# Delta-rule layers: v copied to SBUF by ScalarE, k and q projected to exchanged PSUM banks

## The reference, cut to what matters

```python
def delta_rule(q, k, v, beta):
    def step(W, inp):
        qt, kt, vt, bt = inp
        wk = einsum('bhde,bhe->bhd', W, kt)
        v_new = bt * (vt - wk)
        W = W + einsum('bhd,bhe->bhde', v_new, kt)
        return W, einsum('bhde,bhe->bhd', W, qt)

def fast_ff(x, ln_g, ln_b, slow_w, out_w):
    h = layer_norm(x, ln_g, ln_b)
    q, k, v, beta = split(h @ slow_w.T)          # 8 heads of 64, beta one per head
    q, k, beta = softmax(q), softmax(k), sigmoid(beta)
    return x + delta_rule(q, k, v, beta) @ out_w.T
```

## Time and profile before

| | us |
|---|---|
| median of 3 runs (lowest to highest) | 3078.03 (3076.59 to 3078.49) |
| the profiled execution | 3075.59 |
| its span, first to last instruction | 3073.70 |
| VectorE busy in the span | 2118.2 (69%) |
| TensorE busy in the span | 2422.8 (79%) |
| ScalarE busy in the span | 1209.8 (39%) |
| GpSimd busy in the span | 654.5 (21%) |

### The profile page before, as it was taken

One profiled execution on the slowest core, in us unless ns is written; L12 is line 12 of the kernel. 1 busy time (PEld: TensorE's weight loads), 2 busy tenths in 40 slices (PEclk: granted clock), 3 DMA queues, 4 the chain that ended last, 5 costly groups with the idle time before them and its releaser, 6 DMA issues. The chain is left out here.

```text
span 3073.7 us, 43978 instructions
## 1 busy us (share of the span) xinstructions
PE 2422.8 (79%) x16426; PEld 1407.0 (46%) x16426; DVE 2118.2 (69%) x4507; ACT 1209.8 (39%) x1941; POOL 654.5 (21%) x632
## 2 busy tenths in 40 slices
PE   6757777777659999977888888777688888876598
PEld 2232222222234444335666666543466666665343
DVE  2347888888946777748888888612788888883332
ACT  4555444545423222243444444234343443441332
POOL 0004555555500000022222222101322222220000
PEclk9878888888879999988888988778798989986699
DMA  1000000000010000002222222210122222220000
GB/s 34 1 9 1 0 0 0 1 0 1 0 42 0 0 1 0 26 11 42 42 39 40 36 39 42 39 25 1 32 42 43 43 42 43 43 41 12 16 1 27
DMA packets 280817, 65.88 MB, mean 21 GB/s; under 512 B 272968, under 2 KB 274464, under 8 KB 280224
## 3 DMA queue, kind: packets, MB, share of 16 engines
q1 hardware_dynamic: 280608, 63.09, 11.0%
HBM read 44.20 MB, written 18.86 MB: 21 GB/s over the span
## 5 line engine op out<-in xcount | busy, mean ns | idle before, releaser
L907 POOL TENSOR_TENSOR ma_hc<-ma_state,ma_c 128x508 f32<-128x508 f32 x256 | 302.1, 1183 | 370.9 <-DVE ma_state L994 186.2
L2079 DVE TENSOR_TENSOR fw_lane_x<-fw_lane_x,fw_lane_p 128x126 f32<-128x126 f32 (+22 forms) x992 | 330.6, 333 | 34.0
L994 DVE TENSOR_TENSOR_SCAN ma_state<-ma_da,ma_ps_dbx 128x510 f32<-128x510 f32 x256 | 311.5, 1217 | 32.6 <-issue 24.1
L2075 DVE TENSOR_TENSOR fw_lane_p<-fw_lane_a,fw_lane_x 128x126 f32<-128x126 f32 (+22 forms) x992 | 273.5, 276 | 29.6
L1658 PE MATMUL fw_p<-fw_w,fw_xs 128*127 128x512 f32 (+1 forms) x512 | 238.2, 600 | 54.0 <-DVE fw_qk L2059 26.3
L809 PE MATMUL ma_ps_y<-ma_hc,const 128*128 128x508 f32 x480 | 257.1, 662 | 8.4 <-POOL ma_hc L907 8.4
L989 DVE TENSOR_TENSOR ma_ps_dbx<-ma_ps_b,ma_dtx 128x508 f32<-128x508 f32 x256 | 172.8, 675 | 39.6 <-PE ma_ps_b L793 39.1
L1094 ACT ACTIVATE ex_sig<-ex_gate,ex_gate_scaled 128x508 f32<-128x508 f32 x128 | 87.5, 683 | 271.2 <-PE ex_gate L1064 271.2
L886 ACT ACTIVATE ma_da<-ma_dt,ma_a 128x508 f32<-128x508 f32 x256 | 168.6, 708 | 39.3 <-DVE ma_dt L946 39.2
L793 PE MATMUL ma_ps_b<-ma_bc,select 128*128 128x508 bf16 x128 | 55.7, 435 | 146.5 <-DVE ma_ps_dbx L989 143.1
L1620 POOL TENSOR_TENSOR fw_qk<-fw_qk,fw_masks 128x512 f32<-128x512 f32 x64 | 82.4, 1289 | 403.2 <-ACT fw_qk L1914 403.2
(11 more groups left out here) (304 smaller groups left out, 4898.4 us busy)
## 6 DMA issues: line engine op xcount, KB each, us to landing
fw_lane_a<-fw_a_dram SPq DMA_DIRECT2D x64, 256.0 KB, 4.1
fw_a_dram<-fw_a_t SPq DMA_DIRECT2D x128, 64.0 KB, 2.1
fw_x_dram<-fw_lane_x SPq DMA_DIRECT2D x64, 128.0 KB, 2.9
fw_x_rows<-fw_x_dram SPq DMA_DIRECT2D x128, 64.0 KB, 3.2
fw_x_t<-fw_x_dram SPq DMA_DIRECT2D x128, 64.0 KB, 2.7
x_in<-in_x SPq DMA_DIRECT2D x4, 512.0 KB
ex_gate_up<-in_gate_up SPq DMA_DIRECT2D x1, 2048.0 KB
out<-h SPq DMA_DIRECT2D x1, 2032.0 KB, 6.2
```

Source lines behind the costliest of these rows:

```text
L907: pool.tensor_tensor(two(hc[m % 8][:, :]), state[m % 4][:, :, 1:L + 1], two(c_kept[n % 2][:, :]), ALU.mult).then_inc(s["hc"], 1)
L994: dve.tensor_tensor_scan(line(state[m % 4][:, :, :]), line(da[h][n % 4][:, :, :]), line(dbx[h]), 0.0, ALU.mult, ALU.add).then_inc(s["scan" ...
L2075: dve.tensor_tensor(p, lane_a[:, j:j + 1, j + 1:BLOCK].to_broadcast(shape), lane_x[:, 0:shape[1], j:j + 1].to_broadcast(shape), ALU.mult)\
L2079: dve.tensor_tensor(below, below, p, ALU.subtract).then_inc(inverted[j], 1)
```

## The change

- A new tile `v_rows` in SBUF for each chunk. ScalarE copies the projected v of chunk u into it (`copy_v`, semaphore `v`): `copy_v(0)` after the copy of `k_first`, `copy_v(1)` after `copy_a(1)`.
- `right_hand_side` multiplies `v_rows` with beta, in place of the PSUM bank.
- `sum_qk(1)` waits for `v` in place of `rhs`.
- k is projected and transposed in banks 7 and 3, q is projected in 4 and 5. The projection of k waits for `mask_qk(0)` and the copy of `sum_qk(0)` alone.
- `turn` of k for chunk 1 comes before that of kb for chunk 1 on TensorE; a few waits follow the exchanged banks; ScalarE's exponential of beta waits for `rhs` of the stage before.

```diff
+        v_rows = per("v_rows", [C, NH, D])
-        PROJ_K, PROJ_Q, PROJ_V, BETA = (4, 5), (7, 3), (4, 5), 6
-        TURN_K, TURN_KB, TURN_Q = (4, 5), (6, 7), (3, 6)
+        PROJ_K, PROJ_Q, PROJ_V, BETA = (7, 3), (4, 5), (4, 5), 6
+        TURN_K, TURN_KB, TURN_Q = (7, 3), (6, 7), (3, 6)
...
                     if u == 0:
+                        pe.wait_ge(s["shift_q"], c + 2)
                         pe.wait_ge(s["k_t"], c + 2)
...
-                            pe.wait_ge(s["rhs"], c + 2)
+                            pe.wait_ge(s["v"], c + 2)
...
-                project("k", 0, PROJ_K[0], "qk_even", c)
-                project("k", 1, PROJ_K[1], "qk_copied", c)
+                project("k", 0, PROJ_K[0], "qk_even", max(c - 1, 0))
+                project("k", 1, PROJ_K[1], "qk_copied", max(c - 1, 0))
...
-                turn("kb", 1, kb[1], TURN_KB[1], "kb", "shift_q", c + 1)
                 turn("k", 1, k_rows[1], TURN_K[1], "rows_k", "shift_k", c + 2)
+                turn("kb", 1, kb[1], TURN_KB[1], "kb", "k_t", c + 1)
...
-                turn("q", 0, q_rows[0], TURN_Q[0], "rows_q", "shift_q", c + 2)
+                turn("q", 0, q_rows[0], TURN_Q[0], "rows_q", "k_t", c + 2)
...
+                def copy_v(u):
+                    if prepares:
+                        act.wait_ge(s["proj_v"], c + u + 1)
+                        act.wait_ge(s["rhs"], max(c + u - 1, 0))
+                        act.activation(v_rows[u][:, :, :], heads(bank[0:C, PROJ_V[u], :]), ACT.Copy)\
+                            .then_inc(s["v"], 1)
...
                     act.wait_ge(s["proj_beta"], c + 2)
+                    act.wait_ge(s["rhs"], c)
...
+                copy_v(0)
                 solved(1, 0)
                 copy_a(1)
+                copy_v(1)
                 turned("q", 0, TURN_Q[0], q_t[par][0])
...
-                        dve.wait_ge(s["proj_v"], c + u + 1)
+                        dve.wait_ge(s["v"], c + u + 1)
...
-                        dve.tensor_tensor(rhs[par][u][0:C], heads(bank[0:C, PROJ_V[u], :]), wide(beta[:, u]), ALU.mult)\
+                        dve.tensor_tensor(rhs[par][u][0:C], v_rows[u][:, :, :], wide(beta[:, u]), ALU.mult)\
```

More of the change, by code:

```diff
@@ L1525, in fast_weights @@
             "exp_k", "exp_q", "total_k", "total_q", "recip_k", "recip_q", "rows_k", "rows_q",
-            "beta_exp", "beta_one", "beta", "kb", "rhs", "k_first", "turn_k", "turn_q", "turn_kb", "k_t", "q_t",
+            "beta_exp", "beta_one", "beta", "kb", "v", "rhs", "k_first", "turn_k", "turn_q", "turn_kb", "k_t", "q_t",
             "kb_t", "a_sum", "a_t", "qk_sum", "qk_even", "qk_copied", "qk_odd",
```

## The result

The changed kernel takes 3083.8 us (median; 3082.1 to 3092.7), the kernel before 3076.8 beside it: a ratio of 1.0028, with a 95% interval of 1.0019 to 1.0036. Of the 63 us that VectorE waited on banks at the 28 boundaries the change takes 50 away, and the kernel is 7 us slower. The profiled execution of the changed kernel took 3089.8 us, 6 us above its median.

What follows compares the result with a forecast made beforehand. Two chains of about 8.1 us, VectorE's bank waits and the DMA into `x_rows`, end at `turn_blocks`; the change shortens one. 3075.6 - 4.0 + 13.7 = 3085.3 us, 3087.7 from the median; forecast 3086, range 3066 to 3101.

Steps and rivals of the forecast that it cites:

- the sum: Whole kernel: the profiled 3075.6 us, less 4.0 at the boundaries, plus 13.7 at `rest(0)`, makes 3085.3 us.
- The bank waits: VectorE ahead of `mask_qk(1)` and the first maximum of k: 2.3 us a boundary, to fall to 0.4 to 0.7.
- The 1.4 us in that forecast: From the end of a mask to the first maximum of k: mean taken from the table as 25.6 / 18.
- The DMA chain: Transfers from the inversion's end through `x_rows` to `turn_blocks`: untouched, 8.0 to 8.5 us after the first product; VectorE waits about 2.
- What is gained there: At `turn_blocks`: only what VectorE was late by against the transfers, 4.0 us of the 64 us of bank waits.
- The two first boundaries: First boundary of each layer: 9.34 us against 8.0 to 8.5 for the transfers, a gain of 1.1 each, 2.2 together.
- The 0.15 us each: Boundaries where VectorE didn't wait for transfers: gain estimated from the spread of landings, 12 x 0.15 = 1.8 us.
- The wait at `rest(0)`: VectorE waiting behind TensorE's half clock after the small blocks: mean from 0.96 to 1.45 us, +13.7 us over 28 stages.
- Copies and product: ScalarE's copies of v and VectorE's product from SBUF: cost nil; the rival that they are paid for had 0.13, 3080 to 3105.
- moved together: TensorE's boundary idle time becomes 1 to 3 us ahead of the small blocks; no stage was expected to escape the half clock.
- The rival of a better clock: Projections lose their half clock, no other comes, `rest(0)` follows at once everywhere: 27 us gained, 3047 us; chance 0.10.

Runs made afterwards that it cites:

- the unused matmuls: Changed kernel plus 512-column matmuls whose results nobody reads, three ahead of the wait for `turn_blocks`, one behind `below_blocks`: 3063.8 us, ratio 0.9965.
- both mends: Changed kernel with reads of `lane_a` behind those of `x_rows`, two unread matmuls ahead of the wait for `turn_blocks`, one behind the small blocks: 3032.6 us, ratio 0.9855.

## Why the prediction was right

The forecast was 3086 us, the median 3083.8: +7.0 us between the medians, where the sum had +9.7. The mechanism held; the sizes were in part lucky.

- The bank waits: forecast to go but for 0.4 to 0.7 us. The mask's went, and 0.35 are left ahead of the maximum in 26 of the 28 boundaries (1.63 in the first of each layer). The 1.4 us in that forecast, 25.6 / 18, was misread: it counts four short waits for the second chunk, and the first maximum alone waited 1.28 to 2.23.
- The DMA chain: `turn_blocks` was to stay 8.0 to 8.5 us after the first product, with 2 us of waiting. In the 28 full boundaries it starts 8.07 to 8.73 us after it, 7.98 to 8.65 after the end of the inversion, and waits 2.2 us on average (30.7 / 14).
- What is gained there: forecast 4.0 us, measured 2.8, as the sum over 28 boundaries from the end of the inversion to `turn_blocks` (234.2 us before, 231.4 after). The two first boundaries gave 2.4 of it, as forecast (2.2). The other 26 gave 0.4, not 1.8. The 0.15 us each, taken from the spread of landings, was the weak term.
- The wait at `rest(0)`: forecast a mean of 1.45 us, +13.7 us in all. Measured (18.8 + 21.0) / 28 = 1.42, against (13.4 + 11.9) / 28 = 0.90: +14.5 us. The base was 0.90 over both layers, not the 0.96 of the first. That the mean came so near is luck in part: 1.45 was picked between two stages, and the measured 1.42 is the mean of 11 stages at 0.94 and 17 at 1.73. Its reasons came true: no stage escapes any more (6 did), and the transposes of kb run at half clock, wholly or for the most part, in 25 of 28 stages, where they did in 8.
- Copies and product: forecast nil. The copies alone leave the time at 0.9999. The product from SBUF takes 680 ns, not the estimated 664 (686 from PSUM), so no GpSimd product held it up either:

```profile
L2049 DVE TENSOR_TENSOR fw_rhs<-fw_v_rows,fw_beta 127x512 f32<-127x512 f32 x28 | 17.9, 680 | 0.0
```

By the Trainium skill, "VectorE: DVE Perf Modes", the table in the section on the TRN2 errata, the 64 products would have given back an estimated 4 us. The trace disagrees: 6 ns x 64 = 0.4 us.

The sum of the two terms, -2.8 + 14.5 = +11.7 us, agrees with what the two profiled executions show between the first and the last end of an inversion in the layers: 593.2 and 590.4 us before, 596.3 and 598.7 after, +11.4. That pair differs by 14.2 us as a whole, with 2.6 us already lost in the first 150 us, ahead of all that the change touches. The medians differ by 7.0. So a pair of single executions can be off by as much as the effect itself, and no sum set on one can be trusted to a few us.

Where my account was too short is the clock. I had idle time "moved together" and took a worse clock for the stages behind it. The traces show an exchange: the projections lost their half clock (102.4 to 91.6 us) and the transposes gained it (those of kb 25.6 to 29.5). The half clock costs time by its place: beside a bank wait with a transfer behind it before, in front of `rest(0)` after. The rival of a better clock left no room for what the unused matmuls show: a stage that escapes at one place may pay at the next.

Not settled: why a wait at `rest(0)` of 21.4 us stays when `lane_a` is read later, though the idle time ahead of the small blocks is shorter then. The idle time behind them may be the reason, or that VectorE gets to `rest(0)` earlier: in the kernel before, where TensorE hardly stands ahead of the small blocks (5.5 us in the stretch), the same move lengthened that wait too. No run separates these. Nor was it tried whether useful work could take the place of the unused matmuls.

## What to carry to other kernels

Before a wait is taken away, follow every chain that ends at the same instruction from the same start: here the banks' 8 us lay beside the transfers' 8 us, and 50 us of waits taken away were worth 2.8 there. Then ask where the idle time of the engine that is not the bound goes, for on TensorE the next instructions pay for it. And where two causes lie on one path, try both mends together: here they gave 17 and 20 us alone, and 51 together.

## What the runs showed of the hardware that I had not expected

- Filling one idle stretch can move the half clock to the next. One matmul of 1.12 us behind the small blocks of the kernel before took the wait at `rest(0)` away and cost 25 us, 23.8 us of waits at the state in one layer among it. The Trainium skill, "TensorE: Matmul & The Clock Gate", section "HAM oscillation — how this bites in real kernels", tells of a kernel whose matmuls wait for a transfer in each round, and start each round at the lower clock. The changed kernel agrees in the stage shown: 2.98 us of waiting at `below_blocks`, then 0.50 from 0.4 us into the blocks on.
- Reads of `x_rows` of which the last was issued 1 us earlier took 4.0 us to landing against 3.2, and VectorE waited longer for them. Those of `x_t` came along sooner, and half went by a second queue; which of the two it was stays open. With the reads of `lane_a` behind them, in one queue, it was 2.3. Here the order of the transfers in the queue was worth 17 us, and an earlier issue from two queues cost 18.
